# The first search's index shares: two and six heads instead of four and four

## The reference

```python
q = (x @ Wq + bq).reshape(-1, N_HEADS, D_KEYS)            # 8 heads of 128
s1 = einsum('bhc,hnc->bhn', q1, keys[:, 0])               # two halves, 256 keys each
s2 = einsum('bhc,hnc->bhn', q2, keys[:, 1])
s1t, i1 = top_k(s1, 8); s2t, i2 = top_k(s2, 8)
all_scores = s1t[..., :, None] + s2t[..., None, :]        # 64 sums a head
all_idx = i1[..., :, None] * 256 + i2[..., None, :]
scores, best = top_k(all_scores, 8)
indices = take_along_axis(all_idx, best)                  # 8 experts a head
inner = einsum('bd,bhkd->bhk', x, w_down[indices])
vals = relu(inner) * softmax(scores)
out = einsum('bhk,bhkd->bd', vals, w_up[indices])
```

## Time and profile before

| | |
|---|---|
| median of three runs | 1158.98 us |
| profiled execution | 1159.66 us, span 1157.8 |
| busy, share of the span | PE 94%, DVE 75%, POOL 59%, ACT 38% |
| gathers | 628, of 512 KB each |
| moved over the span | 380 MB, mean 329 GB/s |

### The profile page before, as it was taken

One profiled execution on the slowest core, in us unless ns is written; L12 is line 12 of the kernel. 1 busy time (PEld: TensorE's weight loads), 2 busy tenths in 40 slices (PEclk: granted clock), 3 DMA queues, 4 the chain that ended last, 5 costly groups with the idle time before them and its releaser, 6 DMA issues.

```text
span 1157.8 us, 15265 instructions
## 1 busy us (share of the span) xinstructions
PE 1088.7 (94%) x3706; PEld 578.1 (50%) x3707; DVE 871.9 (75%) x2769; ACT 444.4 (38%) x1091; POOL 684.1 (59%) x758
## 2 busy tenths in 40 slices
PE   7989998489999999999999999999999999998797
PEld 3568887355444454444544544444445444343443
DVE  6747766769989988789798798797798786665411
ACT  3721114444444534434434434434433443441131
POOL 2010005477777777777777776777766777775322
PEclk9989999789999999999999999999999999999899
DMA  8960011499999999999999999999999999976432
GB/s 321 407 260 2 2 40 71 171 411 391 378 410 408 409 409 409 409 409 409 409 409 409 409 409 409 409 409 409 409 407 378 409 409 410 409 307 250 170 107 74
DMA packets 108664, 380.49 MB, mean 329 GB/s; under 512 B 11946, under 2 KB 12624, under 8 KB 108452
## 3 DMA queue, kind: packets, MB, share of 16 engines
q0 software_dynamic: 92352, 334.49, 72.9%
q1 hardware_dynamic: 16228, 45.04, 10.6%
HBM read 352.14 MB, written 28.46 MB: 329 GB/s over the span
## 4 chain that ended last, share of the span: by engine, by line
PE 56%; DVE 18%; DMA 10%; POOL 6%; issue 5%; DVEq 3%; ACT 2%; SPq 0%; POOLq 0%; ACTq 0%
PE tr L2098 26%; DMA big<-in_wdu,idx 10%; PE acc L1878 6%; DVE big L1531 5%; POOL big L701 4%; PE acc L1949 4%; PE tr L2190 4%; PE acc L1990 4%; PE acc L1960 2%; PE acc L1809 2%; POOL AT L701 1%; PE acc L1832 1%; DVE AT L1531 1%; DVE topi L1397 1%; PE tr L1982 1%
## 5 line engine op out<-in xcount | busy, mean ns | idle before, releaser
L701 POOL DMA_INDIRECT big<-in_wdu,idx x504 | 479.6, 952 | 184.9 <-issue 137.7
L2098 PE MATMUL tr<-big,back 128*128 128x512 f32 x1008 | 463.4, 599 | 14.0 <-ACT back L1039 13.6
L1531 DVE CUSTOM_DVE_ANT_0 big<-big,acc,prob 128x512 f32<-128x512 f32 x504 | 353.7, 742 | 82.1 <-DMA big<-in_wdu,idx 80.3
L1039 ACT ACTIVATE back<-ident,inner 128x128 f32<-128x128 f32 x576 | 199.4, 394 | 407.2 <-DVE inner L1531 407.1
L2098 PEld LDWEIGHTS tr<-big,back 128*128 128x128 f32 x1008 | 184.1, 190 | 249.3 <-issue 197.5
L701 POOL DMA_INDIRECT AT<-in_wdu,idx x124 | 118.3, 954 | 40.4 <-issue 34.7
L2098 PE MATMUL tr<-AT,back 128*128 128x512 f32 x248 | 115.1, 598 | 1.4 <-ACT back L1039 1.3
L1531 DVE CUSTOM_DVE_ANT_0 AT<-AT,acc,prob 128x512 f32<-128x512 f32 x124 | 87.3, 742 | 23.2 <-DMA AT<-in_wdu,idx 22.9
L1990 PE MATMUL acc<-front 128*128 128x512 f32 x188 | 90.7, 607 | 0.6 <-issue 0.5
L1878 PE MATMUL acc<-AT,big 128*128 128x256 f32 (+1 forms) x400 | 90.5, 377 | 0.0
L1949 PEld LDWEIGHTS acc<-front 128*128 128x128 f32 x640 | 78.0, 195 | 19.1 <-issue 17.1
(11 more groups left out here) (334 smaller groups left out, 1083.3 us busy)
## 6 DMA issues: line engine op xcount, KB each, us to landing
sorted_rows<-big SPq DMA_DIRECT2D x33, 640.0 KB, 18.7
big<-in_we SPq DMA_DIRECT2D x8, 1024.0 KB, 14.5
big<-in_wdu,idx POOLq DMA_INDIRECT x504, 9.1
x<-sorted_rows SPq DMA_DIRECT2D x14, 257.5 KB, 2.7
x<-in_x SPq DMA_DIRECT2D x1, 2304.0 KB
big<-in_xt SPq DMA_DIRECT2D x2, 1024.0 KB, 8.7
front<-in_wq SPq DMA_DIRECT2D x1, 2048.0 KB, 7.7
AT<-in_wdu,idx POOLq DMA_INDIRECT x124, 9.3
```

The costliest lines, as they stand in the source:

```text
L701: pool.indirect_dma_start(out=k.slot[r * GS + s], out_offset=None, in_=k.wdu_d, in_offset=bass.IndirectOffsetOnAxis(ap=k.idx[i % 2][:, j:j ...
L1039: ins = act.activation(k.diag[:, c * P:(c + 1) * P], to, ACT.Relu, scale=k.inner[:, j:j + 1])
L1531: ins = dve.tensor_tensor_reduce(out=row, in0=row, in1=k.Y[i % 2] if i < NT - 1 else k.Yh[j // WIDTH], scale=k.prob[:, (i % 2) * HK + j:(i ...
L2098: ins = pe.matmul(k.O[i % 2], k.diag[:, c:c + P], row, start=(g == 0 and s == 0), stop=(g == groups_of(i) - 1 and s == GS - 1))
```

## The change

The first share now has two heads and the second six. On VectorE the order becomes pair, part of two heads, pair, pair, pair, part of six heads; `first_part` takes its first and last head instead of a share's number. POOL waits for the second share before group 8 (gather 16) instead of group 16 (gather 32). Shares are still two, and TensorE's and ScalarE's programs are as they were.

```diff
+FIRST_HEADS = 2
...
-            if i == 0 and g and g % (NG // SHARES) == 0:
-                pool.wait_ge(k.idx_ready, g // (NG // SHARES) + 1)
+            if i == 0 and g == FIRST_HEADS * 8 // GS:
+                pool.wait_ge(k.idx_ready, 2)
...
-    def first_part(b):
+    def first_part(h0, h1):
-        hh = H // SHARES
-        at, n = b * hh * 8, hh * 8
+        hh = h1 - h0
+        at, n = h0 * 8, hh * 8
...
-    for b in range(SHARES):
-        first_pair(4 * b)
-        first_pair(4 * b + 2)
-        first_part(b)
+    for h in range(0, FIRST_HEADS, 2):
+        first_pair(h)
+    first_part(0, FIRST_HEADS)
+    for h in range(FIRST_HEADS, H, 2):
+        first_pair(h)
+    first_part(FIRST_HEADS, H)
```

More of the change, by code:

```diff
@@ L1563, in first_part @@
         shape = [P, hh, 8, 8]
-        every = k.all[:, b * hh * 64:(b + 1) * hh * 64]
+        every = k.all[:, h0 * 64:h1 * 64]
         t1 = k.top[:, at:at + n].rearrange("p (h a) -> p h a", h=hh).unsqueeze(3).to_broadcast(shape)
@@ L1571, in first_part @@
         dve.drain()
-        for h in range(b * hh, (b + 1) * hh):
+        for h in range(h0, h1):
             dve.max(k.best[:, h * 8:h * 8 + 8], k.all[:, h * 64:(h + 1) * 64])
         dve.drain()
-        for h in range(b * hh, (b + 1) * hh):
+        for h in range(h0, h1):
             dve.max_index(k.pos[:, h * 8:h * 8 + 8], k.best[:, h * 8:h * 8 + 8], k.all[:, h * 64:(h + 1) * 64])
```

## The result

The changed kernel takes 1165.19 us (median of 7 runs, 1163.57 to 1168.05), the kernel before 1160.06 (median of 7). By the medians it is **5.1 us slower**; the ratio is 1.0048, with a 95% interval of 1.0036 to 1.0060, which is 4.2 to 7.0 us. The forecast was 5.2 us slower.

What follows compares the result with a forecast made beforehand. The prediction took VectorE's end of the first search, which tile 1's search follows, as the bound. Of -5.1 us at the first gather none was kept, of +5.2 on the search all: 1164.2 us, range 1158.5 to 1165.8.

Steps and rivals of the forecast that it cites:

- VectorE's search is the price, not the gathers: The change's price is how much later VectorE ends the first search, not when the first gather starts.
- The sign that the prediction read it from: POOL's first gather of tile 1, at 303.69, waits 2.04 us for tile 1's indices, which VectorE writes.
- The share of two, 3.5 us: First share on VectorE, now two heads, takes 3.5 us; the first gather issues 5.1 us earlier.
- The share of six, 1.55 longer than the second share of before: Second share on VectorE, now six heads, takes 1.55 us longer, at 0.78 per head.
- The stall, about 4 us at full clock: VectorE stands still about 4 us ahead of its last pair, awaiting head 6's score copy; that pair starts 2.23 later.
- The clock, 1.4 us within 0 and 1.9: After a 3.1 us idle, TensorE runs head 5's scores and the queries partly at half rate, adding 1.4 us.
- The search ends 5.2 later: VectorE ends the first search 5.2 us later, between 3.8 and 5.7; tile 1's statistics come near 236.9.
- The early start is spent by gather 20: Gather 20 first reuses a ring place, so POOL waits there for TensorE and none of the 5.1 us is kept.
- POOL's harmless wait for the second share: After 16 gathers, POOL waits some 2 us near 234 for the second share's indices, without harm.
- No slack from there on: From tile 1's first gather, near 308.9, DMA (409 GB/s) and TensorE (99% busy) cannot make up the 5.2 us.
- The absolute time: Forecast of 1164.2 us for the changed kernel, against a median of 1158.98 for the kernel before.
- The rival "the early start is kept": If DMA bandwidth alone set the end, gathers 5.1 us earlier would give 1153.9 us; chance 0.06.

Runs made afterwards that it cites:

- the pause alone: Kernel before, shares of four and four, with 15 maxima of unused results added on VectorE ahead of its last pair: 1165.25 us, ratio 1.0047.
- the two kernels with held gathers: Kernel before, POOL's first gather held until head 5 is found (1161.46 us, ratio 1.0011) or until both index shares are written (1169.13 us, ratio 1.0069).
- the clock held up: Changed kernel with three TensorE products that nothing reads added ahead of head 5's scores: 1164.11 us, ratio 1.0034.

## Why the prediction was right, step by step

- **VectorE's search is the price, not the gathers.** Right: the pause alone costs 5.2 with the gathers where they were, and 5.1 us of earlier gathers without a stall cost or gain nothing. The sign that the prediction read it from was weaker than it took it for: with the gathers held 3.3 us POOL's wait ahead of gather 64 is the same 2.04 us, and the time is 1.4 longer.
- **The share of two, 3.5 us.** 210.01 to 213.57 is 3.56. The first gather is 5.1 us early, as forecast.
- **The share of six, 1.55 longer than the second share of before.** 229.02 to 235.59 is 6.57, against 5.35 (from 223.71, 3.42 after the start of the last pair in the earlier trace rows, to 229.06): 1.2 longer. In the two kernels with held gathers the second share of four takes 5.13 and 5.07, which makes it 1.4 to 1.5. Over-sized by 0.1 to 0.3.
- **The stall, about 4 us at full clock.** 4.02 with the clock held up.
- **The clock, 1.4 us within 0 and 1.9.** 1.46 of the wait. The clock fell in the 3.08 us gap and was back at 0.92 from 220 to 221, so the queries ran partly at each rate, 3.00 us. The Trainium skill's rule ("TensorE: Matmul & The Clock Gate", on HAM oscillation) that a burst behind a wait starts cold agrees with the trace here: 0.50 from 217 to 218. The prediction's upper end of 1.9, the whole burst at half rate, was too high.
- **The search ends 5.2 later.** 5.0 at tile 1's statistics: 3.75 at the last pair (forecast 3.63) and 1.2 from the share.
- **The early start is spent by gather 20.** Right, as was POOL's harmless wait for the second share (1.41, forecast some 2).
- **No slack from there on.** Right in the timings. In the profiled execution gather 64 is 6.2 late, not 5.0. About 1 us of that is TensorE longer at half rate, a term that the prediction lacks: tile 1's queries take 3.78 us (3.45 before) and the first eight instructions for tile 0 4.23 (3.60 before). The profile with the 15 maxima has it too (3.78 and 4.50), the one with the clock held up does not (3.43 and 3.60), though TensorE is idle for 18 us ahead of these queries in both this one and the changed kernel's. The changed kernel's profiled execution is 1.9 us over its median.
- **How close it came.** 5.2 against 5.1 us is closer than the parts deserve: the share was over-sized, the term above was missing, and the measurement leaves 4.2 to 7.0. The chain and the order of its steps came out as forecast; the last tenth is luck.
- **The absolute time** was forecast from a median of 1158.98; with more runs the kernel before has 1160.06, which is why 1164.2 lies 1.0 below 1165.19 while the difference agrees.
- **The rival "the early start is kept"** fell: gathers 5.1 us early were worth nothing. The Trainium skill's rule that HBM is almost always the end-to-end bottleneck ("SBUF — State Buffer", section "A bandwidth-pool intuition that's wrong (but worth ruling out)") does not hold where this change acts; in mid-kernel the trace fits it (409 GB/s), but TensorE is 99% busy there too, and no run tells the two apart. What the prediction did not see is how close that rival is from the other side: held back by more than an estimated 2 to 3 us, the gathers do set the end.

## What to carry to other kernels

Before work is moved out of a gap between two steps of one engine, look up what other engines do meanwhile for the step behind the gap: the share of four looked like a delay of the gathers and was the cover of a chain of 4 us. An earlier start is worth something only if the first thing that it hands over is what the next stage waits for; a ring that fills, or an index that comes later from elsewhere, takes it all back. To see which of two candidates sets the time, delay each by a few us in the old kernel: such runs say more than any share of busy time.

## What the runs showed of the hardware

- The twelve profiles started the first search on VectorE between 202.33 and 206.56 us, with the same code ahead of it. A spread of 4 us ahead of a change is nearly as large as this change's effect, so profiles have to be compared from a common step on, and times by medians of many runs.
- The same kernel (queries of heads 6 and 7 ahead) gave 0.9990 and 1.0007 on two chips, with intervals of 0.1% to either side that barely touch.
- A gap of 3.08 us took TensorE's granted clock from 1.00 to 0.50. Filling a gap with products that nothing reads had it at 1.00 when the next work came, and took 1.46 us off VectorE's wait once, and 2.48 us off the instructions behind the gap once (6.26 to 3.78). The times moved with it, by 1.6 and 1.1 us, but the intervals overlap in both cases.
- A DMA queue that lags behind its issue can hide a delay: with the gathers held by 3.3 us POOL issued gather 64 on time, while the transfers ahead of it landed 9.1 us after their issue instead of 6.9, and the kernel still took 1.4 us more.
